# Mixed rows 0 to 2 of each tile summed in PSUM by VectorE, row 3 in SBUF by ScalarE and GpSimd

## The chip, the cores and the metric

The kernel runs on one core of a Trainium2 chip. A core has TensorE (PE) for matmuls, VectorE (DVE), ScalarE (ACT) and GpSimd (POOL) for element-wise work, and SyncE (SP), which here issues transfers. SBUF is the working memory of 128 partitions, PSUM a smaller memory of eight banks, each 512 floats wide, into which TensorE writes and which VectorE and ScalarE can read and write. GpSimd works in SBUF only. The metric is the device time of one execution in microseconds (us).

## What is computed

Two transformer-like layers on an input of 2 x 512 tokens with 512 channels. Layer 0 is a chunked linear attention and a feed-forward layer, layer 1 an attention followed by the block that the change touches. Of the reference only that block matters. It views the 512 channels of a token as 4 streams of 128, mixes the streams with a 4 x 4 matrix `H_res` of each token (Sinkhorn normalised, 50 iterations), and adds one branch `y`, spread over the streams by `H_post`:

```python
H_res = sinkhorn_log(H_res_logits)
H_pre = jax.nn.softmax(H_pre_logits, axis=-1)
H_post = jax.nn.softmax(H_post_logits, axis=-1)
H_res = (1.0 - g) * I + g * H_res
x_streams = x.reshape(B, T, n, C)              # n = 4, C = 128
x_pre = jnp.einsum('btnc,btn->btc', x_streams, H_pre)
y = x_pre @ W_branch
x_mixed = jnp.einsum('btij,btjc->btic', H_res, x_streams)
y_distributed = jnp.einsum('btc,btn->btnc', y, H_post)
return (x_mixed + y_distributed).reshape(B, T, nC)
# and around it: x = x + gb * (that block)(layernorm(x) * (1 + cb) + sb)
```

## The kernel before

The 1024 tokens are 8 tiles of 128 tokens, one token to a partition, so a tile is 128 x 512 floats. Every engine walks through the same function, `story` (L2360), and each class (`Tensor`, `Vector`, `Scalar`, `Pool`, `Sync`) turns a step into its own instructions or into nothing. The order of the work is thus written out by hand, one list for all engines, and semaphores tie the engines together: a name such as `v_mix` or `g_mix` counts what VectorE or GpSimd has finished.

The end of the program, from about 1471 us on, has three parts.

**The Sinkhorn iteration** (`sinkhorn`, L2158) is a chain of small VectorE instructions that depend on one another, over all tokens at once, with a few `Exp` and `Ln` of ScalarE in it. It ends with `H`, the 4 x 4 matrices of all tokens.

**The branch** (`branch`, L2195) is merged with it. For each tile ScalarE and GpSimd build `x_pre` and TensorE multiplies it by `W_branch` (in banks 0 and 1 of PSUM, in turn). ScalarE copies the result to `yb`, and `rest3` (L1577) multiplies it by `H_post`, one instruction of 128 x 128 for each of the 4 streams, into `mixed[i]`, a tile of 128 x 4 x 128 in SBUF (`mx` in the profile). So before `H` is known `mixed[i]` already holds `y_distributed`.

**The mixing** (`finish`, L2210) begins when `H` is there, and nothing else is left to do by then. Output stream n of tile i gets four products, `H[i, n, k]` times stream k of `hh` (the normalised rows), one token's factor being one number of its partition:

- `mix` (L1268), VectorE: one SCALAR_TENSOR_TENSOR of 128 x 128 that multiplies stream k by the factor and adds it to `mixed[i]` row n, in place. It takes rows 0 and 1 of each tile, and row 2 too in tiles 3 and 7.
- `aside` (L1582 and L1780): for the other rows ScalarE writes the product into `prod` (two buffers in turn, ACTIVATE, L1588), and GpSimd adds it to `mixed[i]` (TENSOR_TENSOR, L1785), two rows in one instruction of 128 x 256, or one row of 128 x 128 in tiles 3 and 7. Each of the four additions waits for the one before it.
- `close` (L1279 and L1787): VectorE multiplies the finished 128 x 512 tile by the modulation `mt` (L1285), GpSimd adds it to the residual `acc` (L1790), and SyncE sends the tile to the output. `close` of tile i-1 stands behind the mixing of tile i on every engine.

Of the kernel before, what the change touches and what calls it, by code (L numbers as in the profile page):

```python
# [8 lines left out]
ALU = mybir.AluOpType  # L9
ACTF = mybir.ActivationFunctionType  # L10
# [3 lines left out]
H, KVH, D, CH = 32, 8, 128, 128  # L14
NT = B * L // 128
# [54 lines left out]
def build(nc, I, out, cst_w):  # L70
# [3 lines left out]
    def sig(name, step=1):  # L74
        return Sig(ctx.enter_context(nc.semaphore(name)), step)

    def dma_sig(name):
        return sig(name, 16)
# [5 lines left out]
    def sb(name, shape, dt=F32):  # L84
        n = int(np.prod(shape[1:])) * sizes[dt]
        t = nc.alloc_sbuf_tensor_at(name, list(shape), dt, offset=place[0])
        place[0] += (n + 31) // 32 * 32
        assert place[0] <= top, (name, place[0], top)
        return t

    pairs = [ctx.enter_context(nc.psum_tensor(f"banks{2 * i}{2 * i + 1}", [128, 1024], F32)) for i in range(4)]
    banks = [pairs[i // 2][:, i % 2 * 512:i % 2 * 512 + 512] for i in range(8)]
# [11 lines left out]
    ve = sb("ve", [128, NT])  # L104
# [5 lines left out]
    acc = sb("acc", [128, NT, 512])  # L110
# [66 lines left out]
    def over(kb, name, shape, dt=F32, end=None):  # L177
        place[0] = base_h + int(kb * 1024)
        t = sb(name, shape, dt)
        assert end is None or place[0] <= base_h + end * 1024, name  # L180
        return t

    past_p = (base_p - base_h) / 1024
    mt = {}
# [43 lines left out]
    for b in range(2):  # L228
# [1 line left out]
            mt[1, blk, b] = over((88, 104)[n // 2] + 4 * (n % 2) + 2 * b, f"mt1{blk}{b}", [128, 512])  # L230
    xp = [over(130 + 0.5 * j, f"xp{j}", [128, 128]) for j in range(2)]
    xpT = [over(131 + 0.5 * j, f"xpT{j}", [128, 128]) for j in range(2)]
    mixed = [over(past_p + 16 + 2 * i, f"mx{i}", [128, 4, 128]) for i in range(NT)]
    yb = [over(past_p + 32 + 0.5 * i, f"yb{i}", [128, 128]) for i in range(NT)]
    prod = [over(past_p + 36 + 2 * j, f"prod{j}", [128, 4, 128]) for j in range(2)]
    place[0] = base_h + 120 * 1024
# [4 lines left out]
    fs = {n_: sb(n_, s_) for n_, s_ in (  # L241
        ("ss", [128, NT]), ("r", [128, NT]), ("lg", [128, NT, 24]), ("W", [128, NT, 4, 4]), ("P", [128, NT, 4, 4]),
        ("T", [128, NT, 4, 4]), ("m", [128, NT, 4]), ("a", [128, NT, 4]), ("b", [128, NT, 4]), ("H", [128, NT, 4, 4]),
        ("hp", [128, NT, 2, 4]), ("hs", [128, NT, 2]))}
# [29 lines left out]
    d_mt = {(blk, b): dma_sig(f"d_mt{blk}{b}") for blk in range(6) for b in range(2)}  # L274
# [10 lines left out]
    v_gt, v_lg, v_sk, v_hp, v_mix, v_rot = [sig(n) for n in ("v_gt", "v_lg", "v_sk", "v_hp", "v_mix", "v_rot")]  # L285
# [4 lines left out]
    a_gt, a_ss, a_hc, a_sk, a_hp, a_xs, a_br, a_mix = [sig(n) for n in  # L290
        ("a_gt", "a_ss", "a_hc", "a_sk", "a_hp", "a_xs", "a_br", "a_mix")]
    g_head, g_rope, g_dec, g_xc, g_stm, g_rs = [sig(n) for n in ("g_head", "g_rope", "g_dec", "g_xc", "g_stm", "g_rs")]
    g_x, g_ln, g_vp, g_rot, g_mix, g_rr, g_pre = [sig(n) for n in ("g_x", "g_ln", "g_vp", "g_rot", "g_mix", "g_rr", "g_pre")]
# [50 lines left out]

    def key_cols(ap):
        return ap.rearrange("p (g c h r) -> p h r g c", g=2, h=2, r=8)

    unit_banks = ((0, 1), (2, 3), (4, 5))

# [19 lines left out]
    class Stages:  # L369
# [40 lines left out]
        aside = mix = close = end = sk_scale = sk_max = sk_sub = sk_exp = sk_sum = sk_ln = sk_inv = sk_mul = sk_add = sk_h = nothing  # L410
# [404 lines left out]
    class Vector(Stages):  # L815
# [452 lines left out]
        def mix(self, i, k, n):  # L1268
            ve, b, j = self.e, i // 4, i % 4
            xs = hh[b][:, j, :].rearrange("p (n c) -> p n c", n=4)  # L1270
            if k == 0:
                ve.wait_ge(*a_mix("o", i, n))
                ve.wait_ge(*v_sk("sk", "H"))
            else:
                ve.wait_ge(*v_mix(i, k - 1, n))
            ve.scalar_tensor_tensor(out=mixed[i][:, n, :], in0=xs[:, k, :], scalar=fs["H"][:, i, n, k:k + 1],  # L1276
                                    in1=mixed[i][:, n, :], op0=ALU.mult, op1=ALU.add).then_inc(*v_mix.up(i, k, n))

        def close(self, i, n0):  # L1279
            ve, o_ = self.e, mixed[i][:, :, :].rearrange("p n c -> p (n c)")  # L1280
            if n0:
                ve.wait_ge(*v_mix(i, 3, n0 - 1))
            ve.wait_ge(*g_mix(i, 3))
            ve.wait_ge(*d_mt[5, i // 4](1))
            ve.tensor_tensor(o_, o_, mt[1, 5, i // 4][:, :], ALU.mult).then_inc(*v_mix.up("close", i))  # L1285


    class Scalar(Stages):
# [288 lines left out]
        def rest3(self, i, m):  # L1577
            ac = self.e
            ac.wait_ge(*a_br("y", i))
            ac.activation(mixed[i][:, m, :], yb[i][:, :], ACTF.Copy, scale=fs["hp"][:, i, 1, m:m + 1]).then_inc(*a_mix.up("o", i, m))  # L1580

        def aside(self, i, k, n0):  # L1582
            ac, b, j, z_ = self.e, i // 4, i % 4, k % 2
            xs = hh[b][:, j, :].rearrange("p (n c) -> p n c", n=4)
            ac.wait_ge(*v_sk("sk", "H"))
            ac.wait_ge(*self.prod_free[z_])
            for n in range(n0, 4):
                ac.activation(prod[z_][:, n, :], xs[:, k, :], ACTF.Copy, scale=fs["H"][:, i, n, k:k + 1]).then_inc(*a_mix.up("x", i, k, n))  # L1588
            self.prod_free[z_] = g_mix(i, k)

        def col_turn(self, bk):
# [5 lines left out]
    class Pool(Stages):  # L1597
# [124 lines left out]
        def key_cols_(self):  # L1722
            po = self.e
            po.wait_ge(*d_a[1]("akv"))
            po.wait_ge(*p_fw("tab", 1))
            for k in range(4):
                for h in range(2):
                    p = po.tensor_copy(kp[:, k, h, :].rearrange("p (r g c) -> p r g c", g=2, r=8), key_cols(akr[:, k, 0:128])[:, h, :, :, :])
            p.then_inc(*g_vp.up("keys"))

        def bias(self, part, bk):
            if part:
                return
            po = self.e
            po.wait_ge(*d_a[2]("ab"))
            for g in range(2):
                for h in range(2):
                    po.tensor_copy(abp[:, 2 * g + h, :].rearrange("p (n r q) -> p n r q", r=8, q=8), wide(ab1[:, 256 * g:256 * g + 256])[:, h, :, :, :])
            for n in range(2):
                for h in range(2):  # L1740
                    p = po.tensor_copy(abp[:, 4 + n, 64 * h:64 * h + 64].rearrange("p (r g c) -> p r g c", g=2, r=8),
                                       key_cols(ab1[:, 512:640])[:, h if n == 0 else 1 - h, :, :, :])
            p.then_inc(*g_vp.up("bias"))
# [33 lines left out]
                po.wait_ge(*p_br("T", i - 2))  # L1777
            po.tensor_tensor(xp[z_][:, :], p_[:, 0, :], p_[:, 1, :], ALU.add).then_inc(*g_pre.up("x", i))

        def aside(self, i, k, n0):  # L1780
            po = self.e
            po.wait_ge(*a_mix("x", i, k, 3))
            if k:
                po.wait_ge(*g_mix(i, k - 1))
            po.tensor_tensor(mixed[i][:, n0:4, :], mixed[i][:, n0:4, :], prod[k % 2][:, n0:4, :], ALU.add).then_inc(*g_mix.up(i, k))  # L1785

        def close(self, i, n0):  # L1787
            po = self.e
            po.wait_ge(*v_mix("close", i))
            po.tensor_tensor(acc[:, i, :], acc[:, i, :], mixed[i][:, :, :].rearrange("p n c -> p (n c)"), ALU.add).then_inc(*g_mix.up("close", i))  # L1790


    class Sync(Stages):
# [167 lines left out]
                inc = d_mr.up(b, qd) if g else d_mr.up(b, qd, 0)  # L1961
                sp.dma_start(qsTs[b][qd // 4][64 * g + 48:64 * g + 50, 2 * (qd % 4):2 * (qd % 4) + 2, :].bitcast(F32), mT[4 * g:4 * g + 4, :].bitcast(F32)).then_inc(*inc)

        def close(self, i, n0):
            sp = self.e
            sp.wait_ge(*g_mix("close", i))
            sp.dma_start(x_out[i], acc[:, i, :]).then_inc(*d_x[i].up("out"))
# [183 lines left out]
    class Sink:  # L2151


        W, P, T, H = (fs[x][:, :, :, :] for x in "WPTH")
        m, av, bv = (fs[x][:, :, :] for x in "mab")
# [52 lines left out]
                E.pre(i0 + j), (yield)  # L2208

    def finish(E):  # L2210
        of = lambda i: 3 if i % 4 == 3 else 2
        for i in range(NT):
            for k in range(4):
                E.aside(i, k, of(i)), (yield)
                for n in range(of(i)):
                    E.mix(i, k, n), (yield)
            if i:
                E.close(i - 1, of(i - 1)), (yield)
        E.close(NT - 1, of(NT - 1)), (yield)

    def layer0_head(E):
        E.load_consts()
# [137 lines left out]
    def story(E):  # L2360
        layer0_head(E)
        layer0_loop(E)
        merged(stream(E, second_front), merged(stream(E, starts, 0), stream(E, weights2))).rest()
        merged(stream(E, parts, 0), stream(E, starts, 1)).rest()
        stream(E, parts, 1).rest()
        E.r_loads()
        E.load_mods()
        pending = joined(stream(E, head, 0), stream(E, mixes, 0))
        attentions(E, pending)
        pending.rest()  # L2370
        stream(E, head, 1).rest()
        E.mix_y(1)
        merged(stream(E, sinkhorn), joined(stream(E, branch, 0), stream(E, branch, 1))).rest()
        stream(E, finish).rest()
        E.end()
# [87 lines left out]
```

## Time and profile before

| what | value |
|---|---|
| median of 3 runs | 1644.7 us (1642.51 to 1648.16) |
| profiled execution, its own time | 1641.26 us |
| profiled execution, span from first to last instruction | 1639.5 us |
| PE, DVE, ACT, POOL busy over the span | 77%, 62%, 39%, 46% |
| start of the mixing | 1591.6 us |
| from there to the end of the span | 47.9 us, 2.9% of it |

The shares of the whole span say little of this change: TensorE is the busiest engine of the program, but its last matmul is long over when the mixing starts. What is to be read is the last stretch, from 1591.6 us on, where VectorE, ScalarE and GpSimd work alone.

### The profile page before, as it was taken

The page shows a single profiled execution, that of the slowest core. Times are in us where ns is not written, and L with a number is a line of the kernel's source. Part 1 is how long each engine was busy: PE and PEld are TensorE (multiplying, and loading weights), DVE is VectorE, ACT ScalarE, POOL GpSimd, SP SyncE. Part 2 cuts the span into 40 slices and gives each one's busy share as a digit, 9 for nine tenths or more (in the row PEclk, how much of TensorE's full clock was granted, in tenths as well). Part 3 has the DMA queues.
Part 4 walks back from the last instruction along what each step waited for, and adds up shares of the span by engine and source line. Part 5 has one row for each costly group of instructions (what it writes and reads, how often), then busy time and mean ns, then how long its engine had stood idle before and what let it go on. Part 6 is the DMA issues. An engine that isn't in the chain of part 4 may idle for free. (4 is left out here: it accounts for less than half of the span.)

```text
span 1639.5 us, 18558 instructions
## 1 busy us (share of the span) xinstructions
PE 1264.2 (77%) x6071; PEld 894.2 (55%) x6071; DVE 1020.0 (62%) x1700; ACT 633.4 (39%) x1198; POOL 756.8 (46%) x742
## 2 busy tenths in 40 slices
PE   2768999999999999999999997659638998940000
PEld 0557776767767768767767775548513334320000
DVE  4644665655565565656556556553446888448898
ACT  0323333433433433334334232352106777733323
POOL 2336656656755756665757565643200012041017
PEclk8889999999999999999999999768858999965555
DMA  5121112122122121121122202201891000000001
GB/s 173 52 61 40 52 56 87 52 71 71 52 78 67 55 72 59 52 65 52 52 71 59 66 12 83 85 1 32 142 154 50 2 2 2 2 1 0 0 0 52
DMA packets 71136, 87.53 MB, mean 53 GB/s; under 512 B 6921, under 2 KB 40873, under 8 KB 70466
## 3 DMA queue, kind: packets, MB, share of 16 engines
q1 hardware_dynamic: 69170, 83.63, 19.3%
q10 hardware_dynamic: 1872, 2.72, 0.4%
q8 instruction: 50, 0.82, 0.2%
q14 instruction: 44, 0.36, 0.1%
HBM read 78.54 MB, written 7.52 MB: 52 GB/s over the span
## 5 line engine op out<-in xcount | busy, mean ns | idle before, releaser
L1161 DVE TENSOR_REDUCE nm<-banks 128x2 f32<-128x1024 f32 x128 | 152.1, 1220 | 50.2 <-PE banks L730 49.5
L1626 POOL TENSOR_TENSOR sw<-sw,sinT 128x512 f32<-128x512 f32 x80 | 103.1, 1289 | 141.6 <-ACT sw L1354 141.6
L1403 ACT ACTIVATE yTh<-yF 128x512 fp32r<-128x512 f32 x64 | 40.4, 632 | 324.3 <-DVE yF L1018 324.3
L1638 POOL TENSOR_TENSOR dec<-gb,gcol 128x512 f32<-128x512 f32 x64 | 70.3, 1099 | 202.4 <-DVE Sd L984 194.7
L1509 ACT ACTIVATE Pb<-banks 128x512 f32<-128x512 f32 x256 | 134.8, 601 | 73.6 <-PE banks L751 73.2
L583 PE MATMUL banks<-st,qt 128*128 128x128 f32 x384 | 82.2, 299 | 52.7 <-DVE Sd L984 27.6
L531 PE MATMUL banks<-hTh,wgh 128*128 128x512 f32 x256 | 121.6, 475 | 0.0
L751 PE MATMUL banks<-qsT,ksT 50*128 50x512 f32 x256 | 90.4, 488 | 36.0 <-DMA qsT<-mT 27.1
L956 DVE SCALAR_TENSOR_TENSOR gs<-tg,banks 128x512 f32<-128x512 f32 x64 | 44.0, 687 | 119.1 <-ACT tg L1361 119.1
L531 PE MATMUL banks<-hTh,wqh 128*128 128x512 f32 x256 | 107.9, 422 | 0.0
L1681 POOL TENSOR_TENSOR acc<-acc,hh 128x512 f32<-128x512 f32 x8 | 10.5, 1315 | 207.3 <-DVE hh L1060 207.3
L611 PE MATMUL banks<-woh,yTh 128*128 128x512 f32 x256 | 103.5, 404 | 0.5 <-DVE yTl L1021 0.5
L584 PE MATMUL banks<-xc,Sd 128*128 128x128 f32 x512 | 97.7, 290 | 4.9 <-DVE Sd L984 4.9
L531 PE MATMUL banks<-hTh,wql 128*128 128x512 f32 x256 | 101.4, 396 | 0.0
L611 PE MATMUL banks<-woh,yTl 128*128 128x512 f32 x256 | 101.0, 395 | 0.0
L531 PE MATMUL banks<-hTl,wqh 128*128 128x512 f32 x256 | 100.7, 394 | 0.0
L611 PE MATMUL banks<-wol,yTh 128*128 128x512 f32 x256 | 100.5, 393 | 0.0
L531 PE MATMUL banks<-hTl,wgh 128*128 128x512 f32 x256 | 100.4, 392 | 0.0
L531 PE MATMUL banks<-hTh,wgl 128*128 128x512 f32 x256 | 100.3, 392 | 0.0
L583 PEld LDWEIGHTS banks<-st,qt 128*128 128x128 f32 x384 | 66.0, 208 | 62.2 <-DVE Sd L984 37.5
L1021 DVE TENSOR_TENSOR yTl<-yF,yTh 128x512 fp32r<-128x512 f32 x64 | 69.8, 1090 | 45.4 <-ACT yTh L1403 45.4
L751 PEld LDWEIGHTS banks<-qsT,ksT 50*128 50x128 f32 x256 | 36.7, 189 | 104.8 <-ACT Pb L1509 39.1
(303 smaller groups left out, 3470.0 us busy)
## 6 DMA issues: line engine op xcount, KB each, us to landing
gb<-g_scr SPq DMA_DIRECT2D x64, 256.0 KB, 3.5
raw<-in_wmod SPq DMA_DIRECT2D x40, 256.0 KB, 2.7
raw<-in_wo SPq DMA_DIRECT2D x32, 256.0 KB, 2.9
raw<-in_wq SPq DMA_DIRECT2D x31, 256.0 KB, 2.7
raw<-in_wg SPq DMA_DIRECT2D x31, 256.0 KB, 2.7
qsT<-q_scr SPq DMA_DIRECT2D x24, 256.0 KB, 9.0
q_scr<-hl SPq DMA_DIRECT2D x32, 128.0 KB, 8.0
mt<-mods_scr SPq DMA_DIRECT2D x12, 256.0 KB, 11.3
```

The lines of the kernel that those rows point to most:

```text
L531: mm = pe.matmul(banks[bk][:, :], w_[:, k, :], x_[:, k, b * 512:(b + 1) * 512], start=(c == 0), stop=(c == 11))
L583: pe.matmul(o, qt[:, h, :], st[:, h, :], start=True, stop=False)
L584: mm = pe.matmul(o, Sd[:, h, :], xc[:, h, :], start=(n == 0), stop=True)
L611: mm = pe.matmul(banks[bO][:, :], y_[:, h, :], w_[:, :], start=(c == 0), stop=(c == 11))
L751: pe.matmul(banks[bk], k_[64 * g:64 * g + 50, p // 4, kt * 128:(kt + 1) * 128], q_[64 * g:64 * g + 50, p % 8, :], start=True, stop=True).t ...
L956: ve.scalar_tensor_tensor(out=gs[t % 2][:, n, :], in0=tg[:, :], scalar=1.0, in1=banks[bk][:, :], op0=ALU.add, op1=ALU.mult).then_inc(*v_ga ...
L1021: ve.tensor_tensor(yTl[:, :, :], yF[:, :, :], yTh[:, :, :].bitcast(F32), ALU.subtract).then_inc(*v_yl.up(s))
L1161: ve.tensor_reduce(nm[:, b, i, p:32:16], pairs[z_][:, :].rearrange("p (g t) -> p g t", g=2), AX.X, ALU.max, negate=True).then_inc(*v_nm.up ...
L1403: ac.activation(yTh[:, :, :], yF[:, :, :], ACTF.Copy).then_inc(*a_yh.up(s))
L1509: ac.activation(Pb[kt % 2][:, 2 * g + pr, :], banks[bk], ACTF.Exp, scale=0.25).then_inc(*a_exp.up(b, qd, kt, pr, g))
L1626: po.tensor_tensor(s_[:, :], s_[:, :], sinT[:, :], ALU.mult).then_inc(*g_rope.up("sin", kind, t, n))
L1638: po.tensor_tensor(dec[:, :, :], gb[s % 2][:, :, :], bc(gcol[:, t % 2, heads(t), n], 2, 128), ALU.subtract).then_inc(*g_dec.up("sub", s))
```

## The change

Rows 0, 1 and 2 of each tile are now summed in a PSUM bank, row 3 in `mixed[i]` in SBUF. A new helper gives the place: `mixed_at(i, n)` is columns 128n to 128n + 127 of bank (i + 2) mod 8 for n < 3, and of `mixed[i]` for n = 3. The banks of eight tiles are all different. `rest3` writes there, and before its very first row waits once until the logits, which used banks 4 to 6, have been read. VectorE does three rows of every tile, in place in PSUM, and its closing multiplication reads 384 columns from PSUM and writes them to `mixed[i]` in SBUF. ScalarE makes one product for each k, GpSimd adds it to row 3 and multiplies row 3 by `mt` itself, so VectorE's closing no longer waits for GpSimd. GpSimd's addition to `acc` stays as it is.

```diff
+    def mixed_at(i, n):
+
+        return (banks[(i + 2) % 8] if n < 3 else mixed[i])[:, n * 128:(n + 1) * 128]
...
         # Vector.mix
-                ve.wait_ge(*a_mix("o", i, n))
+                ve.wait_ge(*a_mix("o", i, 2))
...
-            ve.scalar_tensor_tensor(out=mixed[i][:, n, :], in0=xs[:, k, :], scalar=fs["H"][:, i, n, k:k + 1],
-                                    in1=mixed[i][:, n, :], op0=ALU.mult, op1=ALU.add).then_inc(*v_mix.up(i, k, n))
+            ve.scalar_tensor_tensor(out=mixed_at(i, n), in0=xs[:, k, :], scalar=fs["H"][:, i, n, k:k + 1],
+                                    in1=mixed_at(i, n), op0=ALU.mult, op1=ALU.add).then_inc(*v_mix.up(i, k, n))
         # Vector.close
-            if n0:
-                ve.wait_ge(*v_mix(i, 3, n0 - 1))
-            ve.wait_ge(*g_mix(i, 3))
+            ve.wait_ge(*v_mix(i, 3, 2))
             ve.wait_ge(*d_mt[5, i // 4](1))
-            ve.tensor_tensor(o_, o_, mt[1, 5, i // 4][:, :], ALU.mult).then_inc(*v_mix.up("close", i))
+            ve.tensor_tensor(mixed[i][:, 0:384], banks[(i + 2) % 8][:, 0:384], mt[1, 5, i // 4][:, 0:384], ALU.mult).then_inc(*v_mix.up("close", i))
         # Scalar.rest3
-            ac.activation(mixed[i][:, m, :], yb[i][:, :], ACTF.Copy, scale=fs["hp"][:, i, 1, m:m + 1]).then_inc(*a_mix.up("o", i, m))
+            if i == 0 and m == 0:
+                ac.wait_ge(*v_lg(NT - 1))
+            ac.activation(mixed_at(i, m), yb[i][:, :], ACTF.Copy, scale=fs["hp"][:, i, 1, m:m + 1]).then_inc(*a_mix.up("o", i, m))
         # Scalar.aside
-            for n in range(n0, 4):
-                ac.activation(prod[z_][:, n, :], xs[:, k, :], ACTF.Copy, scale=fs["H"][:, i, n, k:k + 1]).then_inc(*a_mix.up("x", i, k, n))
+            ac.activation(prod[z_][:, 3, :], xs[:, k, :], ACTF.Copy, scale=fs["H"][:, i, 3, k:k + 1]).then_inc(*a_mix.up("x", i, k))
         # Pool.aside
-            po.tensor_tensor(mixed[i][:, n0:4, :], mixed[i][:, n0:4, :], prod[k % 2][:, n0:4, :], ALU.add).then_inc(*g_mix.up(i, k))
+            po.tensor_tensor(mixed_at(i, 3), mixed_at(i, 3), prod[k % 2][:, 3, :], ALU.add).then_inc(*g_mix.up(i, k))
+            if k == 3:
+                po.wait_ge(*g_mix(i, 3))
+                po.wait_ge(*d_mt[5, i // 4](1))
+                po.tensor_tensor(mixed_at(i, 3), mixed_at(i, 3), mt[1, 5, i // 4][:, 384:512], ALU.mult).then_inc(*g_mix.up(i, "scaled"))
         # Pool.close
             po.wait_ge(*v_mix("close", i))
+            po.wait_ge(*g_mix(i, "scaled"))
...
     def finish(E):
-        of = lambda i: 3 if i % 4 == 3 else 2
         for i in range(NT):
             for k in range(4):
-                E.aside(i, k, of(i)), (yield)
-                for n in range(of(i)):
+                E.aside(i, k), (yield)
+                for n in range(3):
                     E.mix(i, k, n), (yield)
```

What VectorE runs at the start of the mixing, before the change. `mx_260` is the SBUF tile of token tile 0, `mx_261` that of tile 1 and so on, `hh_164` holds the streams of tiles 0 to 3 and `hh_165` of 4 to 7, `mt_251` is the modulation.

```order
L1251 TENSOR_SCALAR H<-H,gtc 128x8x4
L1276 SCALAR_TENSOR_TENSOR mx_260<-hh_164,H,mx_260 128x128 x8
L1276 SCALAR_TENSOR_TENSOR mx_261<-hh_164,H,mx_261 128x128 x8
L1285 TENSOR_TENSOR mx_260<-mx_260,mt_251 128x512
L1276 SCALAR_TENSOR_TENSOR mx_262<-hh_164,H,mx_262 128x128 x8
L1285 TENSOR_TENSOR mx_261<-mx_261,mt_251 128x512
L1276 SCALAR_TENSOR_TENSOR mx_263<-hh_164,H,mx_263 128x128 x12
L1285 TENSOR_TENSOR mx_262<-mx_262,mt_251 128x512
```

The same place on VectorE in the changed kernel:

```order
L1255 TENSOR_SCALAR H<-H,gtc 128x8x4
L1280 SCALAR_TENSOR_TENSOR banks<-hh_164,H,banks 128x128 x24
L1287 TENSOR_TENSOR mx_260<-banks,mt_251 128x384
L1280 SCALAR_TENSOR_TENSOR banks<-hh_164,H,banks 128x128 x12
L1287 TENSOR_TENSOR mx_261<-banks,mt_251 128x384
```

The multiply-adds are now 12 to each tile (96 in all, 72 before), with one of their three operands in SBUF and two in PSUM, and the closing is 384 wide with one input in PSUM.

What GpSimd runs for tile 1 and the closing of tile 0, before. `prod_276` and `prod_277` are the two product buffers:

```order
L1785 TENSOR_TENSOR mx_261<-mx_261,prod_276 128x256
L1785 TENSOR_TENSOR mx_261<-mx_261,prod_277 128x256
L1785 TENSOR_TENSOR mx_261<-mx_261,prod_276 128x256
L1785 TENSOR_TENSOR mx_261<-mx_261,prod_277 128x256
L1790 TENSOR_TENSOR acc<-acc,mx_260 128x512
```

The same place on GpSimd in the changed kernel:

```order
L1788 TENSOR_TENSOR mx_261<-mx_261,prod_276 128x128
L1788 TENSOR_TENSOR mx_261<-mx_261,prod_277 128x128
L1788 TENSOR_TENSOR mx_261<-mx_261,prod_276 128x128
L1788 TENSOR_TENSOR mx_261<-mx_261,prod_277 128x128
L1792 TENSOR_TENSOR mx_261<-mx_261,mt_251 128x128
L1798 TENSOR_TENSOR acc<-acc,mx_260 128x512
```

The four additions are half as wide, and one multiplication of 128 x 128 is new between them and the addition to the residual, whose width and place are the same.

## Rows read from the trace of the kernel before

**Rows 1.** Page: the span, and busy tenths in 40 equal slices.

```profile
span 1639.5 us, 18558 instructions
...
DVE  4644665655565565656556556553446888448898
POOL 2336656656755756665757565643200012041017
```

**Rows 2.** Chain that ended last, from 1591 us: start us, us, what.

```profile
1591.28 0.27 DVE H L1251
...
1591.90 2.40 DVE mx L1276 x6
...
1605.98 4.26 DVE mx L1276 x10
...
1634.10 1.64 POOL acc L1790
```

**Rows 3.** Groups from 1591 us: shapes, count, busy us, mean ns, idle before.

```profile
L1276 DVE SCALAR_TENSOR_TENSOR mx<-hh,H,mx 128x128 f32<-128x128 f32 x72 | 36.0, 570 | 0.1
L1785 POOL TENSOR_TENSOR mx<-mx,prod 128x256 f32<-128x256 f32 x24 | 19.9, 829 | 34.3 <-ACT prod L1588 31.7
```

**Rows 4.** Timeline, VectorE and GpSimd at mixing's start: start us, us, engine, xcount.

```profile
1591.64 0.88 DVE L1276 SCALAR_TENSOR_TENSOR mx<-hh,H,mx 128x128 f32<-128x128 f32 x3
...
1593.17 1.07 DVE L1276 SCALAR_TENSOR_TENSOR mx<-hh,H,mx 128x128 f32<-128x128 f32 x2
...
1593.24 0.85 POOL L1785 TENSOR_TENSOR mx<-mx,prod 128x256 f32<-128x256 f32 x1
```

**Rows 5.** One line's instructions: duration ns min/median/max, first and last start.

```profile
L1021 DVE TENSOR_TENSOR yTl<-yF,yTh x64: 692/1164/1173, 127.5 to 1067.3; 128x512 fp32r<-128x512 f32 x64
L1029 DVE TENSOR_TENSOR acc<-acc,banks x56: 674/687/690, 260.9 to 1071.2; 128x512 f32<-128x512 f32 x56
L1018 DVE SCALAR_TENSOR_TENSOR yF<-banks,gnh,gs x64: 729/742/744, 126.1 to 1065.9; 128x512 f32<-128x512 f32 x64
L1185 DVE TENSOR_TENSOR hh<-banks,rd x32: 280/286/292, 1258.5 to 1442.8; 128x128 f32<-128x128 f32 x32
L1245 DVE TENSOR_TENSOR H<-T,b x1: 293/293/293, 1590.6 to 1590.6; 128x128 f32<-128x128 f32 x1
L1778 POOL TENSOR_TENSOR xp<-prod x8: 456/457/542, 1478.2 to 1560.1; 128x128 f32<-128x128 f32 x8
L1790 POOL TENSOR_TENSOR acc<-acc,mx x8: 1258/1302/1642, 1600.4 to 1635.7; 128x512 f32<-128x512 f32 x8
```

**Rows 6.** Timeline: single GpSimd instructions, and two closings of VectorE.

```profile
1599.13 1.21 DVE L1285 TENSOR_TENSOR mx<-mx,mt 128x512 f32<-128x512 f32 x1
1600.42 1.30 POOL L1790 TENSOR_TENSOR acc<-acc,mx 128x512 f32<-128x512 f32 x1 [0.63 <-DVE mx L1285]
...
1607.33 0.50 POOL L1785 TENSOR_TENSOR mx<-mx,prod 128x128 f32<-128x128 f32 x1
1607.97 0.58 POOL L1785 TENSOR_TENSOR mx<-mx,prod 128x128 f32<-128x128 f32 x1
...
1477.43 0.72 POOL L1774 TENSOR_TENSOR prod<-prod 128x256 f32<-128x256 f32 x1 [9.46 <-ACT prod L1560]
1478.23 0.46 POOL L1778 TENSOR_TENSOR xp<-prod 128x128 f32<-128x128 f32 x1
...
1633.35 1.28 DVE L1285 TENSOR_TENSOR mx<-mx,mt 128x512 f32<-128x512 f32 x2
1634.10 2.86 POOL L1790 TENSOR_TENSOR acc<-acc,mx 128x512 f32<-128x512 f32 x2 [1.62 <-DVE mx L1285]
```

**Rows 7.** Timeline of ScalarE, in the Sinkhorn stage and just before the mixing.

```profile
1517.46 0.39 ACT L1580 ACTIVATE mx<-yb,hp 128x128 f32<-128x128 f32 x1
1517.76 0.21 ACT L1546 ACTIVATE b<-b 128x32 f32<-128x32 f32 x1
...
1591.57 0.69 ACT L1588 ACTIVATE prod<-hh,H 128x128 f32<-128x128 f32 x2 [26.04 <-DVE H L1251]
```

More of the change, by code:

```diff
@@ L232, in build @@
     xpT = [over(131 + 0.5 * j, f"xpT{j}", [128, 128]) for j in range(2)]
-    mixed = [over(past_p + 16 + 2 * i, f"mx{i}", [128, 4, 128]) for i in range(NT)]
+    mixed = [over(past_p + 16 + 2 * i, f"mx{i}", [128, 512]) for i in range(NT)]
     yb = [over(past_p + 32 + 0.5 * i, f"yb{i}", [128, 128]) for i in range(NT)]
@@ L1275, in mix, with close @@
                 ve.wait_ge(*v_mix(i, k - 1, n))
-            ve.scalar_tensor_tensor(out=mixed[i][:, n, :], in0=xs[:, k, :], scalar=fs["H"][:, i, n, k:k + 1],
-                                    in1=mixed[i][:, n, :], op0=ALU.mult, op1=ALU.add).then_inc(*v_mix.up(i, k, n))
-        def close(self, i, n0):
-            ve, o_ = self.e, mixed[i][:, :, :].rearrange("p n c -> p (n c)")
-            if n0:
-                ve.wait_ge(*v_mix(i, 3, n0 - 1))
-            ve.wait_ge(*g_mix(i, 3))
+            ve.scalar_tensor_tensor(out=mixed_at(i, n), in0=xs[:, k, :], scalar=fs["H"][:, i, n, k:k + 1],
+                                    in1=mixed_at(i, n), op0=ALU.mult, op1=ALU.add).then_inc(*v_mix.up(i, k, n))
+        def close(self, i):
+            ve = self.e
+            ve.wait_ge(*v_mix(i, 3, 2))
             ve.wait_ge(*d_mt[5, i // 4](1))
-            ve.tensor_tensor(o_, o_, mt[1, 5, i // 4][:, :], ALU.mult).then_inc(*v_mix.up("close", i))
+            ve.tensor_tensor(mixed[i][:, 0:384], banks[(i + 2) % 8][:, 0:384], mt[1, 5, i // 4][:, 0:384], ALU.mult).then_inc(*v_mix.up("close", i))
     class Scalar(Stages):
@@ L1579, in rest3, with aside @@
             ac.wait_ge(*a_br("y", i))
-            ac.activation(mixed[i][:, m, :], yb[i][:, :], ACTF.Copy, scale=fs["hp"][:, i, 1, m:m + 1]).then_inc(*a_mix.up("o", i, m))
-        def aside(self, i, k, n0):
+            if i == 0 and m == 0:
+                ac.wait_ge(*v_lg(NT - 1))
+            ac.activation(mixed_at(i, m), yb[i][:, :], ACTF.Copy, scale=fs["hp"][:, i, 1, m:m + 1]).then_inc(*a_mix.up("o", i, m))
+        def aside(self, i, k):
             ac, b, j, z_ = self.e, i // 4, i % 4, k % 2
@@ L1778, in pre, with aside, close @@
             po.tensor_tensor(xp[z_][:, :], p_[:, 0, :], p_[:, 1, :], ALU.add).then_inc(*g_pre.up("x", i))
-        def aside(self, i, k, n0):
+        def aside(self, i, k):
             po = self.e
-            po.wait_ge(*a_mix("x", i, k, 3))
+            po.wait_ge(*a_mix("x", i, k))
             if k:
                 po.wait_ge(*g_mix(i, k - 1))
-            po.tensor_tensor(mixed[i][:, n0:4, :], mixed[i][:, n0:4, :], prod[k % 2][:, n0:4, :], ALU.add).then_inc(*g_mix.up(i, k))
-        def close(self, i, n0):
+            po.tensor_tensor(mixed_at(i, 3), mixed_at(i, 3), prod[k % 2][:, 3, :], ALU.add).then_inc(*g_mix.up(i, k))
[3 more added lines that the diff above has]
+                po.tensor_tensor(mixed_at(i, 3), mixed_at(i, 3), mt[1, 5, i // 4][:, 384:512], ALU.mult).then_inc(*g_mix.up(i, "scaled"))
+        def close(self, i):
             po = self.e
             po.wait_ge(*v_mix("close", i))
-            po.tensor_tensor(acc[:, i, :], acc[:, i, :], mixed[i][:, :, :].rearrange("p n c -> p (n c)"), ALU.add).then_inc(*g_mix.up("close", i))
+            po.wait_ge(*g_mix(i, "scaled"))
+            po.tensor_tensor(acc[:, i, :], acc[:, i, :], mixed[i][:, :], ALU.add).then_inc(*g_mix.up("close", i))
     class Sync(Stages):
@@ L1962, in max_part, with close @@
                 sp.dma_start(qsTs[b][qd // 4][64 * g + 48:64 * g + 50, 2 * (qd % 4):2 * (qd % 4) + 2, :].bitcast(F32), mT[4 * g:4 * g + 4, :].bitcast(F32)).then_inc(*inc)
-        def close(self, i, n0):
+        def close(self, i):
             sp = self.e
@@ L2210, in finish @@
     def finish(E):
-        of = lambda i: 3 if i % 4 == 3 else 2
         for i in range(NT):
             for k in range(4):
-                E.aside(i, k, of(i)), (yield)
-                for n in range(of(i)):
+                E.aside(i, k), (yield)
+                for n in range(3):
                     E.mix(i, k, n), (yield)
             if i:
-                E.close(i - 1, of(i - 1)), (yield)
-        E.close(NT - 1, of(NT - 1)), (yield)
+                E.close(i - 1), (yield)
+        E.close(NT - 1), (yield)
     def layer0_head(E):
```

## The prediction

> **What bounds the kernel now.** I read the page first, to see which engines live in which stretch: TensorE is done before the end, and in the last slices VectorE is busy 8 and 9 tenths while GpSimd has 0 to 7 [rows 1]. The chain of waits says what sets the end: from the last instruction on `H` at 1591.28 us it stays on VectorE's multiply-adds and closings nearly without a break, until GpSimd's last two additions to `acc` from 1634.10 us on [rows 2]. So here the end of VectorE's work is the end of the program, less a fixed tail. The groups then show that the multiply-adds are dear: 72 of them take 36.0 us busy, 570 ns in the mean, with no idle time before them [rows 3]. And the timeline shows why. The first three, with GpSimd not yet at work, take 0.88 us together [rows 4]: about 0.35 us for one alone and (0.88 - 0.35)/2 = 0.265 us from start to start, since they overlap. From 1593.17 us, with an addition of GpSimd running from 1593.24 us to 1594.09 us, two take 1.07 us, until 1594.24 us [rows 4]: the second could not get through before GpSimd had finished. They meet over and over. Both engines read both of their tensors from SBUF.
>
> That this is about the second SBUF operand is read from other lines [rows 5]. `yTl<-yF,yTh` (two tensors in SBUF) has a minimum of 692 ns and a median of 1164 ns, in a stage where GpSimd works most of the time. `acc<-acc,banks` (one in SBUF, one in PSUM) has 674, 687 and 690 ns over 56 instructions, and `yF<-banks,gnh,gs`, which takes a factor of each partition from SBUF on top, has 729, 742 and 744 ns over 64 [rows 5], in the same loop. With one of the two tensors in PSUM, VectorE is never held up.
>
> **The change, part by part.** The sum is made on the profiled execution: 1641.26 us for a span of 1639.5 us. It is 3.4 us under the median of 1644.7 us, and I carry a gain over unchanged.
>
> *VectorE.* It gets 96 multiply-adds for 72. Their operands are `hh` in SBUF and the bank in PSUM, the kind that is not held up, so I take the pace of the undisturbed ones: 96 x 0.265 = 25.4 us. The closings, two back to back, take 1.28 us, of which one is 0.68 us (the undisturbed length of 512 columns in rows 5, 687 ns), so the pace is 0.60 us for 512 columns. From 512 columns (687 ns) to 128 (286 ns) a column costs 1.04 ns [rows 5], so 384 columns cost 0.13 us less: a pace of 0.47 us and a length of 0.55 us. A tile costs 12 x 0.265 + 0.47 = 3.65 us. The wait on GpSimd at each closing goes. At its pace VectorE would close tile 0 at 1591.64 + 24 x 0.265 + 0.55 = 1598.55 us, tile 1 at 1602.2 us, and tile 7 at 1591.64 + 25.44 + 7 x 0.47 + 0.55 = 1620.9 us.
>
> *GpSimd.* Width 128 alone is 457 ns [rows 5]. An addition that waits for its predecessor and also for ScalarE starts 0.14 us after it (1607.33 + 0.50 to 1607.97) [rows 6]; `xp`, which waits only for its predecessor, starts 0.08 us after it (1477.43 + 0.72 to 1478.23) [rows 6], and I take that for the new scaling, whose other wait has long been over. So a tile takes 0.46 + 3 x (0.14 + 0.46) + (0.08 + 0.46) = 2.80 us, and the addition to `acc`, undisturbed, 1.26 us [rows 5]: 4.06 us. That is more than VectorE's 3.65 us, so **GpSimd becomes the engine that sets the end**, and what it costs is named here: the halving of its additions pays, the scaling (8 x 0.54 = 4.3 us) is on the path. The first two tiles are done by about 1597.6 us, and GpSimd waits for VectorE's closing of tile 0, which reaches it 0.08 us later (1599.13 + 1.21 to 1600.42) [rows 6]: 1598.63 us. Then 1.26 us for `acc` of tile 0, 1599.89 us. Six more rounds: 1599.89 + 6 x 4.06 = 1624.25 us (VectorE's closing of tile 1 at 1602.2 us comes before GpSimd asks for it at 1599.89 + 2.80 = 1602.7 us, and the lead grows). The last addition follows 2.86 - 1.64 = 1.22 us later [rows 6]: 1625.5 us. Before, it ended at 1634.10 + 2.86 = 1636.96 us [rows 6]. **The gain is 11.5 us.** The transfer of the last tile behind it doesn't change.
>
> *ScalarE.* 32 products for 56. It must supply one for each 0.60 us of GpSimd, and two take 0.69 us [rows 7], so it isn't waited for; with two buffers it may begin product k + 2 when addition k has ended, and has 0.14 + 0.46 + 0.14 = 0.74 us for it. `rest3` writes 24 of its 32 rows to PSUM instead of SBUF, which no row shows for any engine but TensorE. The nearest rows are its 0.39 us for SBUF to SBUF; I bound the difference at 0.1 us either way. It is hidden: ScalarE waits 26.04 us before the mixing [rows 7]. Just one of them stands between the `Ln` of `a` and the next instruction that the Sinkhorn chain needs (1517.46 us, the next starts at 1517.76 us) [rows 7], so the edit is worth from -0.1 to 0.1 us, and I take 0. Its new wait for the logits costs nothing, since the Sinkhorn chain needs the same logits before any `rest3`. The order of everything ahead of the mixing is as it was.
>
> *The unknown: VectorE writing PSUM.* No row shows VectorE with its output there. For reading, the rows say that it is free: 286 ns for 128 columns from PSUM (`hh<-banks,rd`), 293 ns with both in SBUF (`H<-T,b`) [rows 5]. I take 0.265 us for the pace, since those are the nearest rows. From below there is nothing to win, because GpSimd sets the pace; a slower VectorE costs nothing up to (4.06 - 0.47)/12 = 0.299 us. At the other end an instruction may not start before the one ahead of it has written: 0.34 us and about 0.035 us between dependent ones, 0.375 us. With pace p the end is 1591.64 + 96p + 3.29 + 0.55 + 0.08 + 1.26 us.
>
> **The rivals.**
>
> *A fixed extra per instruction with PSUM in it.* Between 0.299 us and 0.375 us VectorE sets the end again. At 0.335 us it comes at 1629.0 us, a gain of 8.0 us, so 1636.7 us. For it: the output in PSUM is new. Against it: reading costs nothing extra. The Trainium skill (VectorE: DVE Perf Modes, section on the TRN2 errata) has a table in which an instruction from PSUM pays 120 cycles and one within SBUF 58; at 0.96 GHz an estimate from that is 65 ns more, a pace of 0.33 us and 1636.2 us. The trace does not agree for reading, with the 286 and 293 ns above.
>
> *No overlap of neighbours.* At 0.375 us the end comes at 1632.8 us, a gain of 4.1 us, 1640.6 us: hardly measurable.
>
> *Turns in one bank, slower than before.* Each multiply-add reads and writes the same bank. If that bank serves one of the two at a time, 128 columns cost 0.13 us more, and with neighbours not overlapping the pace is 0.375 + 0.13 = 0.51 us: the end comes at 1645.8 us, a loss of 8.8 us, 1653.5 us. The place is VectorE's 96 instructions, and from a pace of 0.419 us on the kernel is slower. Nothing in the profile shows an engine reading and writing one bank in one instruction; against it speaks that such an instruction in SBUF keeps 0.265 us.
>
> *The change doesn't free the engines of each other.* If GpSimd and VectorE still meet, a tile costs what it does now, (1633.35 - 1599.13)/6 = 5.7 us between the closings of tiles 0 and 6 [rows 6], plus 0.54 us for the scaling and less 0.13 us for the narrower closing, 6.1 us. Eight of them are 48.8 us, where 45.3 us lie between 1591.64 us and 1636.96 us: 1648.2 us. Rows 5 speak against it plainly.
>
> **How the numbers follow.** 0.75 for the forecast, 0.11 for the fixed extra, 0.06 for no overlap, 0.05 for turns in a bank, 0.03 for engines that still meet. The predicted time is 1644.7 - 11.5 = 1633 us. A measurement of this kernel can tell about 0.3%, 4.9 us, from no change. Faster by more than that: 0.75 + 0.11 = 0.86. Within it: 0.06 + 0.03 = 0.09. Slower: 0.05. The range takes in the forecast with the scatter of the three runs (2 us below the median to 3.5 us above) and most of the fixed extra: 1630 to 1638 us.
>
> **What would show it.** In the profile of the changed kernel: multiply-adds at 340 to 350 ns with a maximum close to the median, 12 in about 3.2 us; GpSimd's 128-wide additions at 457 ns, never 0.58 us; the additions to `acc` 4.06 us apart, with no idle time before them after the first; the chain of waits on GpSimd from about 1599 us on; the last addition ending 34 us after the mixing starts. It is wrong if the multiply-adds come more than 0.299 us apart (then the chain stays on VectorE), or if the instructions of the two engines still stretch each other. Were the Sinkhorn stage longer or shorter by more than 0.2 us, PSUM as ScalarE's output would be the cause.

## The result, and the profile after

The changed kernel takes 1633.91 us in the median of 8 runs (1626.9 to 1641.09), the kernel before 1641.74 us in the median of 8 (1635.61 to 1648.76, the three runs shown above among them). The ratio is 0.9941 with a 95% interval of 0.9915 to 0.9967: faster by 0.59%, or 9.7 us, and by 5.4 to 14 us if the interval is carried over. (The ratio is not the quotient of the two medians, which is 0.9952, or 7.8 us.) A later set of rounds gave 0.9918 (0.9888 to 0.9948). The profiled execution has a span of 1633.5 us, 6.0 us less than before.

The page of the profile of the changed kernel, the same lines as in [rows 1]:

```profile
span 1633.5 us, 18589 instructions
...
DVE  4644666656655666555656566654456887636888
...
POOL 2336656666656656766756655653100002031006
```

A 40th of the span is too coarse for this change. What answers is the chain of waits of the changed kernel, from the start of the mixing:

```profile
1598.23 2.23 DVE banks L1280 x9
1600.81 2.74 DVE banks L1280 x11
1604.26 0.47 DVE mx L1287
1604.80 1.26 POOL acc L1798
1606.06 0.42 POOL mx L1788
1606.62 0.47 POOL mx L1788
1607.22 0.46 POOL mx L1788
1607.82 0.46 POOL mx L1788
1608.35 0.46 POOL mx L1792
1608.81 1.22 POOL acc L1798
...
1612.77 1.23 POOL acc L1798
```

Before, this chain was VectorE's nearly to the end [rows 2]. Now it leaves VectorE at the closing of tile 0 and stays on GpSimd: four additions to row 3, the scaling, the addition to the residual, and again, 3.96 us from one addition to `acc` to the next (1608.81 to 1612.77 us). From one dependent addition to the next, wait included, it is 0.60 us (1606.62 to 1607.22 to 1607.82 us).

The instructions of each line of the changed kernel (duration in ns, least/median/most), and behind them the multiply-adds of the kernel before:

```profile
L1280 DVE SCALAR_TENSOR_TENSOR banks<-hh,H,banks x96: 342/346/355, 1598.0 to 1625.3; 128x128 f32<-128x128 f32 x96
L1788 POOL TENSOR_TENSOR mx<-mx,prod x32: 453/456/458, 1598.4 to 1627.6; 128x128 f32<-128x128 f32 x32
L1798 POOL TENSOR_TENSOR acc<-acc,mx x8: 1262/1266/1268, 1604.8 to 1629.8; 128x512 f32<-128x512 f32 x8
L1287 DVE TENSOR_TENSOR mx<-banks,mt x8: 544/546/547, 1604.2 to 1626.0; 128x384 f32<-128x384 f32 x8
```

```profile
L1276 DVE SCALAR_TENSOR_TENSOR mx<-hh,H,mx x72: 337/344/1346, 1591.6 to 1633.1; 128x128 f32<-128x128 f32 x72
```

Not one instruction of either engine is stretched any more. Of the multiply-adds the longest is 355 ns, where the longest was 1346 ns and the mean 570 ns [rows 3]; of the additions the longest is 458 ns, where the timeline had 0.50 and 0.58 us for the same width [rows 6]. The timeline shows their pace, and where the last stretch ends:

```profile
1597.90 0.69 ACT L1591 ACTIVATE prod<-hh,H 128x128 f32<-128x128 f32 x2 [26.05 <-DVE H L1255]
1597.96 1.39 DVE L1280 SCALAR_TENSOR_TENSOR banks<-hh,H,banks 128x128 f32<-128x128 f32 x5
...
1625.56 1.01 DVE L1287 TENSOR_TENSOR mx<-banks,mt 128x384 f32<-128x384 f32 x2
...
1628.58 2.48 POOL L1798 TENSOR_TENSOR acc<-acc,mx 128x512 f32<-128x512 f32 x2
```

Five multiply-adds take 1.39 us, so they come (1.39 - 0.35)/4 = 0.26 us apart. The first 24 of the stage take 6.30 us, the same pace, while GpSimd makes its first eight additions and two scalings. From the first multiply-add to the end of the last addition there are 1628.58 + 2.48 - 1597.96 = 33.1 us, where 45.3 us stood: **12.2 us less**. Counted from ScalarE's first product to the end of the span, which I call the mixing stage from here on, it is 35.6 us for 47.9 us (1639.5 - 1591.57); the spans are given to 0.1 us, so the two counts agree.

The span is only 6.0 us shorter because the mixing starts 6.3 us later than before, at 1597.90 us. That is no cost of the change. The Sinkhorn stage, from VectorE's last logits (`lg`, at 1470.6 us before and 1476.9 us after) to the first product, is 121.0 us in both. What differs lies in the attention of layer 1: its first exponentials come at 1236.2 us before and at 1234.0 us after, so from there to the last logits the changed kernel took 8.6 us longer (242.9 us for 234.4 us). Over the stretch 1236 to 1439 us the columns are: length, busy time and count of PE, PEld, DVE, ACT, POOL, then the granted TensorE clock as a share of full speed, DMA share and GB/s. First the kernel before, then the changed one:

```profile
1236.00:1439.00 203.00, 189.25 (x1148) 78.44 (x1148) 155.56 (x226) 153.74 (x303) 15.36 (x20) 0.97 0.01 2
```

```profile
1236.00:1439.00 203.00, 191.04 (x1117) 77.56 (x1117) 153.16 (x221) 149.22 (x293) 15.38 (x20) 0.93 0.01 2
```

With a clock of 0.97 TensorE gets 1148 matmuls done in it, with 0.93 only 1117. The experiments below show that this goes both ways, whatever the kernel.

### The profile page after: what moved, and what is told of

Read it like the earlier page. It is cut to its first block and busy times, and to the rows that moved or that the text cites. A ratio compares the mean times of both kernels' runs of the same rounds, so it can differ in the third digit from the quotient of the medians.

```text
span 1633.5 us, 18589 instructions
## 1 busy us (share of the span) xinstructions
PE 1274.6 (78%) x6071; PEld 897.4 (55%) x6071; DVE 1008.0 (62%) x1724; ACT 627.6 (38%) x1174; POOL 750.6 (46%) x750
```

## The experiments

All measure the mixing stage in the profile, since it holds what the change touches and was 35.6 us in both profiles of the changed kernel, while the time of a whole execution scatters by several us. Four of the kernels (`old_split_psum`, `before_no_add`, `no_scale`, `more_dve1`) were executed once, in the profile, so nothing is said of their time.

### The same division of work, all in SBUF

```diff
-        return (banks[(i + 2) % 8] if n < 3 else mixed[i])[:, n * 128:(n + 1) * 128]
+        return mixed[i][:, n * 128:(n + 1) * 128]
...
-            ve.tensor_tensor(mixed[i][:, 0:384], banks[(i + 2) % 8][:, 0:384], mt[1, 5, i // 4][:, 0:384], ALU.mult).then_inc(*v_mix.up("close", i))
+            ve.tensor_tensor(mixed[i][:, 0:384], mixed[i][:, 0:384], mt[1, 5, i // 4][:, 0:384], ALU.mult).then_inc(*v_mix.up("close", i))
```

> The division of work of the changed kernel (three rows for VectorE, one for ScalarE and GpSimd, which also scales it), but all four rows in SBUF. The measure is the mixing stage in the profile, from ScalarE's first product to the end of the span: 47.9 us before, 35.6 us with the change. Theory 1, the gain comes from VectorE and GpSimd no longer meeting over two SBUF tensors: here they meet again, VectorE's 96 multiply-adds average above 0.45 us with a maximum of 1.3 us, GpSimd's 128-wide additions go to 0.50 to 0.58 us, and the stage takes 45 us (42 to 47); the time is 0.1 to 0.3% under that of the kernel before. Theory 2, the gain comes from the other division of the rows and of the scaling: the stage takes about 36 us and the time is 0.6 to 0.7% under it.

Measured: the mixing stage takes 48.5 us, and the ratio to the kernel before is 1.002 (0.9998 to 1.0042). The whole gain is gone, and the stage is 0.6 us longer than before the change. The multiply-adds average 491 ns. The instructions of this kernel (ns, least/median/most):

```profile
L1280 DVE SCALAR_TENSOR_TENSOR mx<-hh,H,mx x96: 335/342/1346, 1592.7 to 1635.0; 128x128 f32<-128x128 f32 x96
L1788 POOL TENSOR_TENSOR mx<-mx,prod x32: 496/580/586, 1593.1 to 1633.6; 128x128 f32<-128x128 f32 x32
```

one tile of its timeline:

```profile
1623.90 0.55 DVE L1287 TENSOR_TENSOR mx<-mx,mt 128x384 f32<-128x384 f32 x1
1624.37 5.30 DVE L1280 SCALAR_TENSOR_TENSOR mx<-hh,H,mx 128x128 f32<-128x128 f32 x12
1624.53 1.30 POOL L1798 TENSOR_TENSOR acc<-acc,mx 128x512 f32<-128x512 f32 x1 [1.22 <-DVE mx L1287]
1625.79 2.67 POOL L1788 TENSOR_TENSOR mx<-mx,prod 128x128 f32<-128x128 f32 x4
...
1629.59 0.54 DVE L1287 TENSOR_TENSOR mx<-mx,mt 128x384 f32<-128x384 f32 x1
```

and a piece of its chain of waits:

```profile
1629.07 0.60 DVE mx L1280 x2
```

Twelve multiply-adds take 5.30 us, where 0.26 us apart they would take 3.2 us, and the tile is 5.69 us long. That settles that the other division of the rows and of the scaling gains nothing without PSUM: theory 2 falls. The whole gain takes both, as the next experiment shows. My 45 us for theory 1 was 3.5 us too low, outside the 42 to 47 us, and the time, which I had put 0.1 to 0.3% under that of the kernel before, came out at the same or a little above. I had taken the pattern of tile 3 of the kernel before and let VectorE finish its twelve within GpSimd's work. It doesn't: when GpSimd is through with its additions and the scaling, at 1629.0 us, two multiply-adds still follow (1629.07 to 1629.67 us), and GpSimd stands idle for the closing, 1.22 us in the tile shown.

### PSUM, but the rows divided as before

```diff
+    of = lambda i: 3 if i % 4 == 3 else 2
...
-        return (banks[(i + 2) % 8] if n < 3 else mixed[i])[:, n * 128:(n + 1) * 128]
+        return (banks[(i + 2) % 8] if n < of(i) else mixed[i])[:, n * 128:(n + 1) * 128]
...
         # Pool.aside
+            m_, w = mixed[i][:, 128 * of(i):512], 128 * of(i)
+            po.tensor_tensor(m_, m_, prod[k % 2][:, of(i):4, :].rearrange("p n c -> p (n c)"), ALU.add).then_inc(*g_mix.up(i, k))
...
+                po.tensor_tensor(m_, m_, mt[1, 5, i // 4][:, w:512], ALU.mult).then_inc(*g_mix.up(i, "scaled"))
```

ScalarE makes both products again where two rows are left to it, and VectorE's closing is as wide as its rows (256 or 384 columns).

> PSUM for VectorE's rows as in the changed kernel, but with the division of before: two rows for VectorE (three in tiles 3 and 7), the rest for ScalarE and GpSimd, which scales what it summed. Theory 1 (no meeting, and then the busier engine sets the end): GpSimd needs 5.3 us for a tile of two rows and 4.0 us for one row, so the mixing stage takes 42.8 us (42 to 44), with VectorE's multiply-adds undisturbed at 0.35 us and VectorE idle before its closings or done early. Theory 3, PSUM alone is the gain whoever does the rows: about 36 us.

Measured: 43.0 us. The groups of this kernel (shapes, count, busy us, mean ns, idle before):

```profile
L1282 DVE SCALAR_TENSOR_TENSOR banks<-hh,H,banks 128x128 f32<-128x128 f32 x72 | 19.2, 344 | 0.1
L1793 POOL TENSOR_TENSOR mx<-mx,prod 128x256 f32<-128x256 f32 x24 | 17.4, 724 | 34.3 <-ACT prod L1594 31.7
L1803 POOL TENSOR_TENSOR acc<-acc,mx 128x512 f32<-128x512 f32 x8 | 10.0, 1261 | 0.0
```

Nothing is stretched here either (344 and 724 ns, where 570 and 829 ns stood in [rows 3]), and yet only 4.9 of the 12.2 us are there. GpSimd's additions to `acc` have no idle time before them: from its first addition on it has no break but the short starts between dependent instructions, and it sets the end. So PSUM frees the engines, and the way from 43.0 us to 35.6 us is made by giving VectorE, which it has freed, the third row. The 4.9 us are PSUM and the moved scaling together: GpSimd scales its own rows here, 5.2 us of work (6 instructions of 723 ns and 2 of 454 ns) that it didn't have before. What PSUM would be worth with the scaling left to VectorE was not measured.

### The kernel before without the additions to the mixed rows

```diff
         # Vector.close
-            ve.wait_ge(*g_mix(i, 3))
+            ve.wait_ge(*a_mix("o", i, 3))
         # finish
-                E.aside(i, k, of(i)), (yield)
```

> The kernel before with ScalarE's products and GpSimd's additions to the mixed rows left out (rows 2 and 3 of a tile, row 3 in tiles 3 and 7, keep only the branch); everything of VectorE and GpSimd's additions to the residual stay, all in SBUF. Theory 1: the multiply-adds were long because of GpSimd's additions; now their median is 0.34 us and they are held only by the additions to the residual, once for each tile, about 1.0 us. 72 x 0.265 + 8 x 0.60 + 7 x 1.0 = 30.9 us, and with the tail the stage from the first multiply-add takes about 36 us. Rival: multiply-adds in place in SBUF are slow by themselves (a latency that PSUM hasn't): their mean stays near 0.57 us and the stage near 47 us.

Measured: 34.6 us from the first multiply-add (1594.47 us) to the end of the span (1629.1 us), 1.4 us under my 36 us, where the kernel before takes 47.9 us. The multiply-adds, still in place in SBUF, average 425 ns and have a median of 340 ns. Two pieces of this kernel's timeline:

```profile
1594.47 4.29 DVE L1276 SCALAR_TENSOR_TENSOR mx<-hh,H,mx 128x128 f32<-128x128 f32 x16
1598.68 0.68 DVE L1285 TENSOR_TENSOR mx<-mx,mt 128x512 f32<-128x512 f32 x1
1599.28 3.19 DVE L1276 SCALAR_TENSOR_TENSOR mx<-hh,H,mx 128x128 f32<-128x128 f32 x8
...
1599.44 1.30 POOL L1790 TENSOR_TENSOR acc<-acc,mx 128x512 f32<-128x512 f32 x1 [36.01 <-DVE mx L1285]
```

The first sixteen, with GpSimd silent, come (4.29 - 0.34)/15 = 0.26 us apart. The next eight, with one addition to `acc` beside them, take 3.19 us instead of 2.2 us: 1.0 us lost to an addition of 1.30 us. The rival, that such an instruction is slow in SBUF by itself, falls. ScalarE's products are left out here as well, but they are not what held VectorE up: the kernel before begins with three multiply-adds at full pace while ScalarE's products run (from 1591.57 us) and GpSimd's additions don't yet [rows 4, rows 7], and here VectorE is held up beside GpSimd alone.

### The changed kernel without the scaling of row 3

```diff
-            if k == 3:
-                po.wait_ge(*g_mix(i, 3))
-                po.wait_ge(*d_mt[5, i // 4](1))
-                po.tensor_tensor(mixed_at(i, 3), mixed_at(i, 3), mt[1, 5, i // 4][:, 384:512], ALU.mult).then_inc(*g_mix.up(i, "scaled"))
...
-            po.wait_ge(*g_mix(i, "scaled"))
+            po.wait_ge(*g_mix(i, 3))
```

> The changed kernel without GpSimd's scaling of row 3 (left out: row 3 of each tile isn't multiplied by the modulation). Theory 1 with GpSimd as the engine that sets the end at 3.97 us a tile: without 0.53 us it needs 3.44 us, VectorE needs 3.57 us and takes over, and the mixing stage takes 32.4 us (32 to 33) instead of 35.6 us. If VectorE set the end already, the stage stays at 35.6 us.

Measured: 33.3 us, 2.3 us less than with it and 0.3 us above my range, and in the middle of the stage the chain is VectorE's again (a tile is 3.57 us, 1618.32 to 1621.89 us):

```profile
1618.32 0.46 DVE mx L1287
1618.78 2.40 DVE banks L1280 x10
1621.29 0.10 DVE banks L1280
1621.54 0.35 DVE banks L1280
1621.89 0.46 DVE mx L1287
```

So GpSimd's scaling is on the path of the changed kernel. Most of the 0.9 us that I missed stands at the end of this kernel's timeline:

```profile
1632.49 1.01 DVE L1287 TENSOR_TENSOR mx<-banks,mt 128x384 f32<-128x384 f32 x2
...
1633.13 2.48 POOL L1794 TENSOR_TENSOR acc<-acc,mx 128x512 f32<-128x512 f32 x2
```

VectorE closes tiles 6 and 7 one right behind the other, and GpSimd's last addition to row 3 ends at 1633.17 us, so both additions to `acc` are left to do after that, and I had counted one.

### One multiply-add more for each tile

```diff
         # Vector.close
+            for j_ in range(1):
+                ve.wait_ge(*v_mix(i, 3, 2) if j_ == 0 else v_mix("more", i, j_ - 1))
+                ve.scalar_tensor_tensor(out=banks[(i + 2) % 8][:, 384:512], in0=hh[i // 4][:, i % 4, 0:128], scalar=fs["H"][:, i, 0, 0:1],
+                                        in1=mixed_at(i, 0), op0=ALU.mult, op1=ALU.add).then_inc(*v_mix.up("more", i, j_))
```

> The changed kernel with one more multiply-add of VectorE for each tile, into columns 384 to 511 of the tile's bank, which nobody reads. Theory 1, GpSimd sets the end and VectorE has 0.40 us to spare for each tile: only the first closing comes later by one or two of them, so the mixing stage takes 35.9 us (35.6 to 36.2). If VectorE set the end: 8 x 0.26 = 2.1 us more, 37.7 us.

Measured: 35.9 us. Eight more instructions of 0.26 us, 2.1 us of VectorE's time, cost 0.3 us together. VectorE has the time to spare that the sum said.

### The changed kernel again, and the scatter ahead of the mixing

> The changed kernel once more, unchanged, for a second profile and more rounds. In the first pair of profiles the mixing stage was 12.2 us shorter, but the span only 6.0 us, because the attention of layer 1 ahead of it took 6.3 us longer. Theory 1, that part is scatter that the change has nothing to do with: the mixing stage is again 35.6 us (to 0.2 us) and the Sinkhorn stage 121.0 us, the attention lands anywhere in the spread of the other kernels' profiles, and the ratio over all rounds comes to about 0.993 (12 us of 1643 us). Rival, the change makes the attention slower (its code there is the same, but semaphore counts and addresses may act): the mixing begins at 1597 us or later again, and the ratio stays at 0.994 to 0.996.

Measured: a mixing stage of 35.6 us, a Sinkhorn stage of 121.0 us, a span of 1623.6 us, and a ratio of 0.9918 (0.9888 to 0.9948). The mixing began at 1588.0 us this time, 3.6 us earlier than in the profile of the kernel before. Over all nine profiles, whose code ahead of `rest3` is the same, it began anywhere from 1586.7 us to 1604.8 us, and the order follows the clock granted in this stretch: 1586.7 to 1591.6 us in the three with 0.97, 1592.6 to 1596.6 us in the three with 0.95, 1597.6 and 1597.9 us in the two with 0.93, and 1604.8 us in the one with 0.90. That latest was the kernel without the scaling:

```profile
1236.00:1439.00 203.00, 187.87 (x1086) 77.54 (x1087) 154.12 (x220) 144.24 (x283) 15.35 (x20) 0.90 0.03 11
```

The earliest was the kernel of the next experiment, with 0.97:

```profile
1236.00:1439.00 203.00, 188.70 (x1144) 76.97 (x1136) 152.63 (x225) 150.37 (x296) 15.46 (x21) 0.97 0.01 2
```

So the 6.3 us of the first pair are scatter, and it goes with the granted clock of TensorE in the attention, though not all of it: part of the latest start was there before the exponentials began (the first at 1242.1 us, against 1236.2 us before). What made the clock differ from one execution to the next, no run here shows. Both ratios have 0.9926 in their intervals, which is what 12.2 us of 1641.74 us make.

### The last tile on VectorE

```diff
+    of = lambda i: 4 if i == NT - 1 else 3
...
         # finish
-                E.aside(i, k), (yield)
-                for n in range(3):
+                if of(i) < 4:
+                    E.aside(i, k), (yield)
+                for n in range(of(i)):
                     E.mix(i, k, n), (yield)
-            if i:
+            if 0 < i < NT - 1:
                 E.close(i - 1), (yield)
+            if i == NT - 2:
+                E.close(i), (yield)
```

> The changed kernel with all four rows of the last tile in PSUM on VectorE (ScalarE and GpSimd mix nothing of it), and with the closing of tile 6 ahead of the mixing of tile 7. GpSimd loses 2.7 us of its chain, VectorE gets 4 x 0.26 + 0.13 = 1.2 us, and both then end together. Theory 1, with the measured paces: the addition of tile 6 ends 1.2 us after that of tile 5, VectorE closes tile 7 about 29.8 us after its first multiply-add, and the mixing stage takes 33.6 us instead of 35.6 us. If the last tile's length doesn't count, 35.6 us. In the time 2 us of 1633 us are at the edge of what the rounds can tell.

Measured: 33.8 us (33.6 us expected), 1.8 us less than the changed kernel, a span of 1620.5 us, and a ratio to the kernel before of 0.9913 (0.9887 to 0.994). Its median of 6 runs was 1627.97 us, that of the changed kernel in the same rounds 1627.37 us: the 1.8 us are seen in the stage only, not in the time. The fourth row on VectorE and the earlier closing of tile 6 were not tried apart. The timeline of the end:

```profile
1611.69 4.24 DVE L1282 SCALAR_TENSOR_TENSOR banks<-hh,H,banks 128x128 f32<-128x128 f32 x16
1615.96 0.69 DVE L1289 TENSOR_TENSOR mx<-banks,mt 128x512 f32<-128x512 f32 x1
...
1613.36 2.48 POOL L1801 TENSOR_TENSOR acc<-acc,mx 128x512 f32<-128x512 f32 x2
1616.73 1.26 POOL L1801 TENSOR_TENSOR acc<-acc,mx 128x512 f32<-128x512 f32 x1 [0.88 <-DVE mx L1289]
```

VectorE finishes last by 0.9 us, so what is left to shift between the two is less than that. It is the shortest mixing stage of the kernels here that compute everything.

## Why the prediction came out, point by point

**What bounds the kernel** held: VectorE, stretched by GpSimd over two tensors in SBUF. The kernel all in SBUF and the one without the additions say so from two sides. That the second tensor in SBUF was the condition had been read from other lines [rows 5], and it carried over to an instruction that no row had shown. The experiments put input and output into PSUM together; that the input alone is enough is said only by the lines of [rows 5] whose output is in SBUF.

**VectorE's 96 multiply-adds** were put at 0.265 us apart and came 0.26 us apart. The open step, VectorE writing into PSUM, cost nothing: 346 ns for 0.35 us alone in SBUF [rows 4]. In the second profile of the same kernel they have 350 to 372 ns, above the 340 to 350 ns that I had named as a sign, but with the maximum still close to the median and the stage as long. With a pace of 0.26 us the fixed extra, the lack of overlap and the turns in a bank are out. By the table of the Trainium skill (VectorE: DVE Perf Modes, section on the TRN2 errata) an instruction from PSUM to SBUF costs 62 cycles more than one within SBUF (120 against 58), an estimated 65 ns at its 0.96 GHz. The closings are such a pair, and they don't bear it out: 546 ns for 384 columns from PSUM, 545 ns for the same closing in the kernel all in SBUF. For an output in PSUM that table has no column.

**The closings** were put at a length of 0.55 us and measured 0.546 us (0.567 us in the second profile).

**GpSimd as the engine that sets the end** held, shown by the chain, by the kernel without the scaling and by the one with more for VectorE. A tile was put at 4.06 us and took 3.96 us: the first addition of a tile, which waits for nothing on its engine, starts 0.04 us before the one ahead of it has ended and costs 0.42 us, not 0.46 us, and so does the addition to `acc`, 1.22 us for 1.26 us. Over the six rounds the 0.10 us make 0.6 us, most of what the stage came out shorter (33.1 us for 33.8 us, a gain of 12.2 us for 11.5 us).

**ScalarE** was hidden as said: the Sinkhorn stage kept its 121.0 us. Writing to PSUM it was 34 ns faster than writing to SBUF, within the 0.1 us.

**The time**: 1633 us was forecast and 1633.91 us measured, but the nearness is partly luck. The forecast stood on a median of three runs, 1644.7 us, and with eight the kernel before has 1641.74 us. What the sum can be held to is the ratio: 1633/1644.7 is 0.993, and the intervals around 0.9941 and 0.9918 both hold it. That the first pair of profiles shows 6.0 us and the stage 12.2 us was not forecast; I had named the scatter of the runs but not that much of it sits in the attention and that from one execution to the next it is as large as the gain.

## What to carry to other kernels

Where VectorE and GpSimd work side by side, look at the spread of the durations of one VectorE line: a median near the least with a most several times as long (337/344/1346 ns here) says that some of its instructions are held up, not that they are slow. The cure here was to take one of VectorE's two tensors out of SBUF, and a free PSUM bank is a place to accumulate in, even when TensorE has no part in it. Then divide the work anew, because the freed engine has time (here the way from 43.0 us to 35.6 us came from that), and measure in the stage, since a gain of 12 us is no larger than the spread of the whole (1635.61 to 1648.76 us for the kernel before).

## What the runs showed of the hardware

- VectorE adding in place in a PSUM bank (one input and the output there, the other input and the factor in SBUF) takes 342 to 355 ns for 128 columns in one profile and 350 to 372 ns in another of the same kernel, and comes 0.26 us apart, the same as in SBUF, with neighbours in the same bank. That was the largest unknown of the forecast.
- ScalarE's Copy with a factor, 128 columns, SBUF to PSUM and SBUF to SBUF in the same profile:

```profile
L1584 ACT ACTIVATE banks<-yb,hp x24: 352/356/366, 1494.2 to 1571.2; 128x128 f32<-128x128 f32 x24
L1584 ACT ACTIVATE mx<-yb,hp x8: 386/390/393, 1495.9 to 1571.5; 128x128 f32<-128x128 f32 x8
```

- The hold-up costs GpSimd too: its 128-wide addition has a median of 580 ns beside VectorE with two tensors in SBUF, 456 ns beside VectorE with one in PSUM.
